# Cross-attention with a mixture of experts: the attention stage's PE, ACT and DVE lists in a new order

## What is computed

```python
q = _ln(_fp8_linear_pertensor(ln_out, wq, wq_scale, q_in_scale).reshape(b, s, g, hpg, d), qln_w, qln_b)
k = _ln(_fp8_linear_pertensor(ln_out, wk, wk_scale, k_in_scale).reshape(b, s, g, d), kln_w, kln_b)
v = _fp8_linear_pertensor(ln_out, wv, wv_scale, v_in_scale).reshape(b, s, g, d)
core = _gqa(q, k, v).reshape(b, s, nh * d)      # scores, softmax, values
# qx, kx, vx, xout: the same, with kx and vx from the context
catq = _div_clamp_fp8(jnp.concatenate([core, xout], axis=-1), proj_smooth)
return jnp.einsum('bsi,oi->bso', catq, wproj) * (proj_in_scale * proj_w_scale)
```

## Time and profile before

| | before |
|---|---|
| median of three runs | 1134.46 us (1134.02 to 1134.89) |
| profiled execution, its own time | 1130.54 us |
| its span, first to last instruction | 1128.6 us |
| mean granted TensorE clock | 0.958 |
| PE busy | 989.4 us, 88% |
| DVE busy | 824.0 us, 73% |
| ACT busy | 716.1 us, 63% |
| POOL busy | 405.8 us, 36% |
| PE busy from 143.19 to 722.53 us | 552.52 of 579.34 us |

### The profile page before, as it was taken

One profiled execution on the slowest core, in us unless ns is written; L12 is line 12 of the kernel. 1 busy time (PEld: TensorE's weight loads), 2 busy tenths in 40 slices (PEclk: granted clock), 3 DMA queues, 4 the chain that ended last, 5 costly groups with the idle time before them and its releaser, 6 DMA issues. The chain is left out here.

```text
span 1128.6 us, 23597 instructions
## 1 busy us (share of the span) xinstructions
PE 989.4 (88%) x7206; PEld 692.6 (61%) x7207; DVE 824.0 (73%) x1596; ACT 716.1 (63%) x1223; POOL 405.8 (36%) x627
## 2 busy tenths in 40 slices
PE   2447999999999999999999999958999959999994
PEld 1434667667676667666676766746565536666663
DVE  6566888988888888888889888878866634444442
ACT  5967777777777777777777777636455515445452
POOL 3005444444444444444444444400561002332332
PEclk8679999999999999999999999986999979999998
DMA  9245110000100101001010010013453146222222
GB/s 278 50 92 170 43 39 19 27 29 19 37 19 19 37 19 37 19 19 37 19 37 19 19 37 19 1 57 131 150 188 130 56 150 132 28 23 28 28 24 27
DMA packets 32369, 65.20 MB, mean 58 GB/s; under 512 B 3664, under 2 KB 20688, under 8 KB 31952
## 3 DMA queue, kind: packets, MB, share of 16 engines
q1 hardware_dynamic: 23312, 50.20, 13.7%
q0 software_dynamic: 9024, 14.59, 7.6%
HBM read 53.42 MB, written 16.59 MB: 62 GB/s over the span
## 5 line engine op out<-in xcount | busy, mean ns | idle before, releaser
L754 POOL TENSOR_TENSOR root<-vareps,neghalf 128x4 f32<-128x4 f32 (+1 forms) x128 | 169.0, 1320 | 10.0
L747 POOL TENSOR_TENSOR var<-ssq,unit 128x4 f32<-128x4 f32 (+1 forms) x128 | 50.0, 391 | 314.6 <-DVE ssq L659 314.6
L543 PE MATMUL b_pj<-w_hi,xq 128*128 128x512 f16 x384 | 146.6, 382 | 6.6 <-PEq L154 6.3
L559 PE MATMUL b_tr<-ident,nrm 128*128 128x128 f32 x768 | 120.6, 280 | 35.7 <-ACT qT L629 17.4
L543 PE MATMUL b_pj<-w_lo,xq 128*128 128x512 f16 x384 | 146.5, 382 | 0.0
L659 DVE TENSOR_REDUCE ssq<-sq 128x4 f32<-128x512 f32 x192 | 128.5, 681 | 14.9 <-ACT sq L611 14.8
L670 DVE TENSOR_TENSOR nrm<-raw,rstd 128x512 f32<-128x512 f32 x192 | 126.4, 686 | 16.2 <-POOL rstd L758 14.5
L1321 POOL DMA_INDIRECT out<-xg x39 | 60.6, 1553 | 210.7 <-ACT xg L1422 191.4
L559 PEld LDWEIGHTS b_tr<-ident,nrm 128*128 128x128 f32 x768 | 85.5, 146 | 73.0 <-DVE nrm L670 41.0
L569 PEld LDWEIGHTS b_sc<-kT,qT 128*128 128x128 f32 x1024 | 124.3, 192 | 9.3 <-ACT qT L629 0.3
L569 PE MATMUL b_sc<-kT,qT 128*128 128x64 f32 x1024 | 121.3, 272 | 0.0
(11 more groups left out here) (258 smaller groups left out, 2260.8 us busy)
## 6 DMA issues: line engine op xcount, KB each, us to landing
nst<-in_ffw SPq DMA_DIRECT2D x30, 512.0 KB, 3.3
wload<-in_ffw SPq DMA_DIRECT2D x30, 512.0 KB, 3.4
xbuf<-zero SPq DMA_DIRECT2D x39, 129.0 KB, 2.5
xg<-xbuf SPq DMA_DIRECT2D x9, 516.0 KB, 4.2
w<-in_w_all POOLq DMA_DIRECT2D x12, 256.0 KB, 9.2
x_sb<-in_x SPq DMA_DIRECT2D x4, 512.0 KB, 6.8
cstage<-in_ctxT SPq DMA_DIRECT2D x1, 2048.0 KB, 9.6
w<-in_w_all SPq DMA_DIRECT2D x4, 512.0 KB, 14.8
```

The lines of the kernel that those rows point to most:

```text
L543: last = pe.matmul(o, a[:, k, bass.ts(i, P)], w[:, k, at:at + BANK], start=(k == 0 and n_ == 0), stop=(k == KT - 1 and n_ == len(terms) - 1))
L559: last = pe.transpose(o, nrm[:, c, hd * P:(hd + 1) * P], ident[:, :])
L754: pool.tensor_tensor(root[:, r % 2, c, :], vareps[:, r % 2, c, :], neghalf[:, 0:1].unsqueeze(2).to_broadcast(shape), ALU.pow).then_inc(s[" ...
```

## The change

The functions stay what they are, but for three things. `act_raw(c)` is cut in two: `act_square(c)` and the copy, each a step of its own. Since a bank may now be copied before it is squared or the other way round, `pe_project` waits for both, so c = 0, 2 and 3 have one more semaphore wait. `dve_stats` moves from unit N - 2 to N - 3, so the tail has one more slot. Then the lists of PE, ACT and DVE have a new order; POOL's and SP's are untouched.

```diff
-                for N in range(4 * (NT - 1), 4 * NT + 2):
+                for N in range(4 * (NT - 1), 4 * NT + 3):
                     slot(N // 4, N % 4)
...
                     after(pe, "raw_done", n - 1)
+                    if c != 1:
+                        after(pe, "sq_done", NN * (4 * i + r) + max(c - 1, 0))
...
+            def act_square(c):
+                def step(act, i, r):
+                    N = 4 * i + r
+                    m = NN * N + c
+                    act.wait_ge(s["proj_done"], 4 * N + c + 1)
+                    after(act, "ssq_done", m - 1)
+                    act.activation(sq[:, (r * NN + c) % 2, :], b_pj[c % 2][:, :], ACT.Square).then_inc(s["sq_done"], 1)
+                return step
...
-                        m = NN * N + c
-                        after(act, "ssq_done", m - 1)
-                        act.activation(sq[:, (r * NN + c) % 2, :], bk, ACT.Square).then_inc(s["sq_done"], 1)
-                        after(act, "norm_done", m - 2 * NN + 1)
+                        after(act, "norm_done", NN * N + c - 2 * NN + 1)
...
-                run_slots(pe, [(1, pe_scores), (2, pe_transpose(0)), (3, pe_project(0)), (3, pe_project(1)), (2, pe_transpose(1)), (0, pe_probT), (-1, pe_values), (2, pe_transpose(2)), (3, pe_project(2)), (-2, pe_out), (3, pe_project(3))])
...
-                run_slots(act, [(2, act_tev(0)), (1, act_exp), (3, act_raw(0)), (3, act_raw(1)), (2, act_tev(1)), (0, act_ptev), (2, act_tev(2)), (0, act_weight_squares), (3, act_raw(2)), (3, act_raw(3))])
```

More of the change, by code:

```diff
@@ L764, in _ @@
             def _(pe):
-                run_slots(pe, [(1, pe_scores), (2, pe_transpose(0)), (3, pe_project(0)), (3, pe_project(1)), (2, pe_transpose(1)), (0, pe_probT), (-1, pe_values), (2, pe_transpose(2)), (3, pe_project(2)), (-2, pe_out), (3, pe_project(3))])
+                run_slots(pe, [
+                    (1, pe_scores),
+                    (2, pe_transpose(0)),
+                    (3, pe_project(0)),
+                    (3, pe_project(1)),
+                    (0, pe_probT),
+                    (2, pe_transpose(1)),
+                    (3, pe_project(2)),
+                    (-2, pe_out),
+                    (2, pe_transpose(2)),
+                    (-1, pe_values),
+                    (3, pe_project(3)),
+                ])
             @block.scalar
             def _(act):
-                run_slots(act, [(2, act_tev(0)), (1, act_exp), (3, act_raw(0)), (3, act_raw(1)), (2, act_tev(1)), (0, act_ptev), (2, act_tev(2)), (0, act_weight_squares), (3, act_raw(2)), (3, act_raw(3))])
+                run_slots(act, [
+                    (2, act_tev(0)),
+                    (3, act_square(0)),
+                    (3, act_raw(0)),
+                    (3, act_square(1)),
+                    (1, act_exp),
+                    (2, act_tev(1)),
+                    (3, act_square(2)),
+                    (3, act_raw(1)),
+                    (3, act_raw(2)),
+                    (2, act_tev(2)),
+                    (3, act_raw(3)),
+                    (0, act_ptev),
+                    (0, act_weight_squares),
+                ])
             @block.vector
@@ L775, in early @@
                     moments(dve, range(EARLY))
-                run_slots(dve, [(1, dve_max), (1, dve_sub), (2, dve_norm(1)), (2, dve_norm(2)), (3, dve_squares(0)), (3, dve_squares(1)), (1, dve_sum), (1, dve_recip), (1, dve_prob), (-1, dve_cat), (-1, dve_clip), (-1, dve_round), (3, dve_squares(2)), (3, dve_norm(0)), (-2, dve_residual), (-2, dve_stats)], early)
+                run_slots(dve, [
+                    (2, dve_norm(1)),
+                    (1, dve_max),
+                    (1, dve_sub),
+                    (2, dve_norm(2)),
+                    (3, dve_squares(0)),
+                    (3, dve_squares(1)),
+                    (1, dve_sum),
+                    (1, dve_recip),
+                    (3, dve_squares(2)),
+                    (1, dve_prob),
+                    (3, dve_norm(0)),
+                    (-2, dve_residual),
+                    (-1, dve_cat),
+                    (-1, dve_clip),
+                    (-3, dve_stats),
+                    (-1, dve_round),
+                ], early)
                 dve.wait_ge(s["st3_done"], NT)
```

## The result

The changed kernel takes 1094.86 us (median of 4 runs, 1094.46 to 1095.90); the kernel before, beside it on the same chip, takes 1134.26 us (4 runs, 1134.02 to 1134.89). The ratio is 0.9661, 95% interval 0.9645 to 0.9677. Forecast were 1094.5 us, 1088 to 1112.

A forecast was written before the change was run, and what follows sets the result against it. The attention block was taken as nearly bound by PE, DVE close behind: 59 slots x 0.68 us waiting = 40 us, head and tail cancelling, so 1130.54 becomes 1090.5, plus 3.9 to the median gives 1094.5 us; range 1088 to 1112.

The forecast's parts named there:

- The period without waits: Attention block's steady part: PE alone needs 9.07 and 9.89 us in alternating slot kinds, mean 9.48 against 10.16 before.
- The waits on nrm and on the evacuation: PE in the kind-0 slot: 0.79 us lost ahead of transpose 1, 0.22 ahead of transpose 2; both would go.
- the 40: Gain in us over the steady part: 59 slots, each 0.68 us of PE waiting shorter.
- small gaps of 0.05 and 0.08: PE around transpose 1 and probT: may go with the wait, at most 8 us, which would give 1087.
- the first wait: PE's 0.79 us ahead of transpose 1: squares 2 stands late on DVE behind cat, clip and round; chain through POOL 3.90 us.
- The layout of ACT: ACT's new list in a kind-0 slot: every evacuation, square and copy in time, the tightest, copy 0, by 0.35 us.
- The semaphore waits: Further waits ahead of projects 0, 2 and 3 on PE: taken as 0, at most 14 us (1108.5).
- (a): DVE and POOL form a 9.8 us ring, 0.32 above PE: 1113 us; chance 0.28, together with dearer semaphore waits.
- (b): Late sub on DVE delays exp on ACT, holding three banks and transpose 2: 10 us slower, 1144 us; chance 0.06.
- (c): No change: waits of the same size move to places counted as covered, nearest copy 0 to project 2; 1134 us, chance 0.04.
- (d): PE without rest in the steady part would run at a lower clock; given no chance.
- The tail: End of the attention block: values(62) stands behind out(61), which waits for round; residual at 24.5 instead of 23.5 us, 1 lost.

The follow-up runs named there:

- the old lists: Changed kernel with PE, ACT and DVE lists in the old order, keeping the further sq_done waits and extra tail slot: 1134.51 us, ratio 1.0011 to the kernel before.
- The kernel with values first: Changed kernel with PE's old order of values ahead of out in the last slots alone, from slot 62 on: 1086.32 us, ratio 0.9610 to the kernel before.
- the power on POOL: Changed kernel with one more power of 4 columns on POOL between squares 2 and norm 1, result unread: 1125.99 us, ratio 0.9957 to the kernel before.
- the small sum: Changed kernel with one more addition of 8 columns on POOL between squares 2 and norm 1, result unread: 1093.25 us, ratio 0.9666 to the kernel before.
- norm 2 first: Changed kernel with norm 2 moved ahead of max and sub on DVE: 1096.10 us, ratio 0.9668 to the kernel before.
- the two kernels in which PE waits 2 to 2.6 us in most slots: Kernel before with only DVE's list new: 1304.08 us, ratio 1.1503; changed kernel with ACT's list old: 1339.34 us, ratio 1.1791 to the kernel before.

## Why the prediction was right

**The period without waits.** Forecast were slots of 9.07 and 9.89, mean 9.48; measured 9.01 and 9.87, mean 9.44. The waits on nrm and on the evacuation are gone. Of the 2.6 us beyond the 40, about 0.7 is the slot of before, 10.17 us in this stretch and not 10.16, and 1.9 is PE's list, 9.45 us a slot where 9.48 was laid out. Of the small gaps of 0.05 and 0.08, which the prediction had left open up to 8 us and counted at nothing, that ahead of values did not go: it moved with values and stands behind transpose 2 (422.07 - 421.54 = 0.53, where a transposition otherwise takes 0.44 to the next step). PE busy over 98% of the steady part was to show it; it is 100%. Two figures of the text are loose without effect on the sum: 10.09 - 0.79 - 0.22 is 9.08 and not 9.07, and the "three and a half microseconds" from squares 2 to norm 1 are the 3.90 that the layout uses.

**Where the first wait came from.** That squares 2 stood late is borne out: put back late, together with norm 0, it costs 2.1 us a slot. The chain through POOL did not stay at 3.90 us but took 4.31 to 4.48; of the 0.41 more in the slot shown, 0.32 is vareps, counted at its old length, and the rest about rstd. It hurt nobody, since norm 1 at 1.47 had until 3.65.

**The layout of ACT.** Each bank was in time as worked out, project 2 behind copy 0 too: no wait of a project matmul on ACT stands among PE's waits. The layout holds only as a whole: PE's, ACT's or DVE's list alone cost 48, 25 and 171 us against the kernel before, the changed kernel without PE's or ACT's costs 24 and 205, and all three together give 39. That refutes the rival that each list has a share of its own. The pair of PE's and ACT's lists with DVE's old one was not run; the nearest to it, squares 2 and norm 0 back in their late place, stands 88 us above the kernel before.

**The semaphore waits.** The prediction counted them at nothing, between bounds of 0 and 14 us. The ratio with the old lists leaves at most 2.6 us. With the new lists project 2 starts 0.44 behind transpose 1 (410.36 - 409.92), with its further wait, just as project 0 followed transpose 0 before without it.

**The rivals.** (a) This was the right bound to look at, but mis-sized: blocking adds 0.4 to 0.6 us to the ring and not up to 1.3, since var comes through between prob and norm 0, which follow each other on DVE without idle time. The ring is about 9.0 us, not 9.8. The Trainium skill (SBUF — State Buffer, section "Who interferes with whom") has DVE instructions with two SBUF inputs, and some with one in a faster mode, shut GpSimd out until they end. The trace agrees: var, vareps and rstd end within 0.06 us of prob, norm 0 and round. The Trainium skill makes the order of issue decide who blocks whom, but that section has nothing on who is next when POOL's step has waited and DVE goes on at once; here it is POOL, in every slot of the steady part (var of 8 columns takes 580 ns on the mean, 582 at most). (b) Sub starts at 2.8 in the slot and could start 0.6 later without effect. (c) and (d) did not come: no wait turned up on PE, and its clock stayed at 1.00 in the steady part.

**The terms that were mis-sized.** The tail cost 4.7 us where I wrote 1: I worked through the order, but with the lengths of the full clock. In the window of the tail it is 0.82, before 0.93 (722.53 to 747.00), and values takes 2.03 and 2.08 where the earlier trace rows has 1.16. The four slow steps of the tail are 3.4 us longer than at a clock of 1.00, and without that the tail would be 28.3 - 3.4 = 24.9 us, near the 24.5 forecast (an estimate). The kernel before had slow steps there too, behind a wait, but only some 1.6 us of them (with probT, 1.06 instead of 0.60):

```profile
726.53 1.11 PE L559 MATMUL b_tr<-ident,nrm 128*128 128x128 f32 x4 [1.67 <-DVE nrm L670]
...
728.43 1.85 PE L588 MATMUL b_o<-probT,v 64*128 64x128 f32 x16
```

The kernel with values first gets the order and the clock back at once, so a run that separates the two is missing. The tail cost 3.7 us more than forecast and the steady part gave 2.6 more, so that the two errors nearly cancel, and part of the hit is luck. The 2.3 us in the experts' part don't follow the lists: from the last residual to the end of the span are 382.5 us in the profiled execution before and 386.4 with all lists old, 382.4 with the power on POOL, and 384.9, 384.5, 385.8 and 383.6 in the changed kernel and those with the small sum, with norm 2 first and with values first. The execution of before was a short one there, which the forecast took up as the 3.9 us between it and the median. Why single executions differ by so much in that part is open.

## What to carry to other kernels

Engines that work through fixed lists form rings; lay out a whole turn for every engine with start times from the timeline before moving a step, and move the lists together, since one moved alone can cost more than the whole gain. When PE has become the bound, the length of the next ring says how much is left to put on it: here some 0.4 us a slot. The drain of such a loop wants its own order, since there latency counts and no longer PE's time; it gave another 0.6% (1086.32 against the 1093.25 us of the kernel with the small sum).

## What the runs showed of the hardware

A GpSimd instruction of 0.20 us can be held by a DVE instruction with two SBUF inputs, but gets in between two that follow each other: from the start of prob at 402.92 to the end of norm 0 at 404.20 DVE is busy throughout, and var, held first, is through at 403.66. Each of the three short steps pays for one DVE instruction and no more (0.58, 0.52, 0.33 us); round, which holds the third, has one input, of 16 bits. In the two kernels in which PE waits 2 to 2.6 us in most slots, the out behind such a wait ran at PE's lower clock in 53 of 61 cases (0.91 and 0.89 on the mean of the stretch, a transposition 1.06 instead of 0.60 us); behind a wait of 1.48 us in the same loop it didn't. So a late step cost more than its wait there: slots of 12.96 and 13.51 us where I had worked out 12.2 for either at the full clock. Waits on semaphores that are long satisfied, three more a slot, cost PE nothing that 12 runs could show (1.0011, 0.9998 to 1.0023).
